# ScalarE issues half of the spreads of five norms' scales, and half of the first quarter's values in the first chunk

## The chip, the core and the metric

The kernel runs on one core of a Trainium2 chip. The metric is the device time of one execution in microseconds. The names of the engines in what follows are the profile's: PE (TensorE, matmuls) with PEld (its weight loads), DVE (VectorE), ACT (ScalarE), POOL (GpSimd), and SP (SyncE), which does no arithmetic here and issues the DMAs. "SPq" is SP's instruction queue: the time that its instructions take there.

## The reference

The input is x with 16 sequences of 512 tokens and 128 channels. A block with a recurrent attention (16 heads of 8 channels) and a feed-forward net is added to it, and then a small mixture of four experts:

```python
x = x + attn_block(_layernorm(x))
x = x + ffn_block(_layernorm(x))

# in attn_block
x = _ln(x, ln_pre_w, ln_pre_b)
xn = _ln(x, ln_attn_w, ln_attn_b)
r, k, v = xr @ W_r, xk @ W_k, xv @ W_v      # xr, xk, xv: xn mixed with its shift by one token
kk = kk / norm(kk)
def step(state, inp):                       # 512 steps, one after the other
    sa = einsum('bhij,bhj->bhi', state, a_t)
    state = state * d_t + sa * b_t + v_t * k_t
    return state, einsum('bhij,bhj->bhi', state, r_t)
x = x + (_gn_heads(o) + bonus) * g @ W_o
xf = _ln(x, ln_ffn_w, ln_ffn_b)
x = x + square(relu(kf @ W_ffn1)) @ W_ffn2

# in ffn_block: each token goes to the expert with the largest logit
y = _layer_norm(gelu(x @ W1[e] + b1[e]) @ Wo + bo + x)
```

## The kernel before

**Layout and chunks.** Channels lie on the 128 partitions. The 512 tokens are cut into 16 chunks of 32 steps. A chunk has 32 x 16 = 512 columns (step, sequence), and a step of the scan works on 8 x 16 = 128 columns.

**The order of the work.** Each engine's program is written out by hand. The tables `AT`, `AT_FIRST` (the first two chunks) and `AT_LAST` (the last two) give every piece of a chunk's work a place, counted in scan steps of that chunk: places below 0 lie in the iteration before, places from 32 on in those behind. In iteration i the engines scan chunk i, prepare chunk i+1 and finish chunks i-1 and i-2. At each step t an engine takes the scan's own instruction first and then, in `others()`, what the tables put there, the later chunk ahead of the earlier one. Every engine is strictly in order: an instruction that waits holds up all that stands behind it.

**A scan step.** DVE multiplies the state by `a_t` (`s_a`, L884), PE sums that over each head into `sa_ps` (L405), DVE multiplies the sums by `b_t` (`upd`, L894) and adds `plus_kv` (`state`, L898). POOL makes `plus_kv` (L1071) and multiplies the states by `r_t`. The products `kv` of keys and values are made by DVE (L871) eight steps ahead, one quarter of the chunk (8 steps) at a time, out of `val_rep0` and `val_rep1`, in which each value stands on all partitions of its head.

**PE's own filler.** Beside the needed matmuls PE runs the `keep` matmuls (L586), whose result nobody reads.

**The norms' scales.** A norm's variance is summed by PE in `sums` (L361) into a quarter of a bank, 32 partitions for each quarter of the columns. ACT makes the scale out of it with Ln and Exp on a tile of 128 x 128 (`rsqrt_row`, L618 and L620, the tile `row[name]`). Four DMAs, one for each quarter, then copy the 32 partitions to all 128 of `rs_p`, `rs_m` or `rs_f` (`over_channels`, L301). DVE multiplies by that. The norms are `rs0` and `rs1` (ahead of the attention, chunk i+1 in iteration i), `frs` (ahead of the feed-forward net, chunk i-1), `ers` (chunk i-1) and `lrs` (the experts' two, `lrs` of chunk i-2). `rk`, the scale of the keys, is spread in the same way (L298). The scale of the per-head norm of the scan's output is made by ACT in full width instead (`rs_m`, L609 and L611, the place `grs`) and needs no DMA.

**The values.** `replicate` (L314) issues eight DMAs for a quarter: each copies the 16 partitions of one value index of `val_c` to all 128.

**The queue of DMAs.** Every DMA is issued by SP, in order. In an iteration SP takes: the load of x, the values of quarters 1 and 2 of chunk i, the scales rs0 and rs1 (chunk i+1) and frs (chunk i-1), the values of quarter 3, rk, the values of quarter 0 of chunk i+1, the second load of x, lrs, ers and the store.

The lines that the prediction speaks of besides these: on ACT the decay's tanh (`dec_bt`, L679) and the tanh of `th_a` (`dx`, L683); the squares of the feed-forward net's hidden layer (`hid`, L757); the evacuations `val_c` (L696) and `val` (L701). On DVE the mix for the gate (`mix_g`, L926), which `th_a` waits for; the product with the per-head norm's scale (`y_m`, L962, the place `gxh`). On PE the first layer of the experts (`fin_a`, `fin_b`, L564) and the second layer of the feed-forward net (`mid_ps`, L515).

Of the kernel before, what the change touches and what calls it, by code (L numbers as in the profile page):

```python
# [13 lines left out]
H, N = 16, 8  # L14
# [4 lines left out]
QCOLS = QUARTER * B  # L19
# [93 lines left out]
class Chunk:  # L113


    def __init__(self, base, off):
        self.base, self.off = base, off
        self.slot = off % RING
        self.place = AT_FIRST if off < 2 else AT_LAST if off >= CHUNKS - 2 else AT

    def __add__(self, n):
        return Chunk(self.base, self.off + n)
# [18 lines left out]
def settled(eng, value):  # L141

    return value if isinstance(value, int) else eng.to_reg(value)


def build(nc, xT, mats, vecs, consts, b1_in, out):
    with ExitStack() as ctx:
        def sb(name, cols, dtype=F32, rows=128):
            return ctx.enter_context(nc.sbuf_tensor(name, [rows, cols], dtype))
# [4 lines left out]
        def single(name, cols):  # L154
            return [sb(name, cols)] * RING
# [4 lines left out]
        def sem(name):  # L160
            return ctx.enter_context(nc.semaphore(name))
# [31 lines left out]
        val_rep = [sb(f"val_rep{n}", N * QCOLS) for n in range(2)]  # L193
        val_scan = sb("val_scan", C)
        val_c = sb("val_c", COLS)
# [3 lines left out]
        sq_p, rs_p, xh_p = (sb(n, COLS) for n in ("sq_p", "rs_p", "xh_p"))  # L199
        row = {n: sb(f"row_{n}", QCOLS) for n in ("rs0", "rs1", "rk", "frs", "ers", "lrs")}  # L200
# [6 lines left out]
        rkb, kk, kki, inv_p, th_a = mix["k"], mix["v"], mix["g"], dec_bt, dx  # L207
# [7 lines left out]
        x2, sq_m, rs_m, y_m, z_m = (sb(n, COLS) for n in ("x2", "sq_m", "rs_m", "y_m", "z_m"))  # L215
# [3 lines left out]
        y1, y1b, y2, sq_f, rs_f = (sb(n, COLS) for n in ("y1", "y1b", "y2", "sq_f", "rs_f"))  # L219
        h = single("h", COLS)  # L220
# [25 lines left out]
        s = {n: sem("s_" + n) for n in names}  # L246
# [14 lines left out]
        def pipeline(eng, work, scan_step=None):  # L261

            def iteration(c):
                for t in range(STEPS):
                    def others():
                        for skew in range(-FIRST, CHUNKS - LAST - 2, -1):
                            if (c + skew).has():
                                work(c + skew, t - skew * STEPS)
                    if scan_step:
                        scan_step(c, t, others)  # L270
                    else:
                        others()

            for c in range(FIRST, LAST + 1):
                iteration(Chunk(0, c))


        @block.sync
        def _(sp):
            sp.dma_start(x_in[0][:], xT[:, 0:COLS]).then_inc(s["x_in"], 16)  # L280
            sp.dma_start(con[:], consts).then_inc(s["consts_in"], 16)
            sp.dma_start(vec[:], vecs).then_inc(s["consts_in"], 16)
            sp.dma_start(mat[:], mats).then_inc(s["w_in"], 16)
            sp.wait_ge(s["tiles"], 1)
            for n in range(3):
                sp.dma_start(b1_rows[32 * n:32 * n + E, :], b1_in).then_inc(s["b1_in"], 16)

            def over_channels(c, name, to, free=(), heads=None):

                waits = [(s[n], settled(sp, (c + back).count())) for n, back in free if c.has(-back)]  # L290
                now = settled(sp, c.count())
                for done, n in waits:
                    sp.wait_ge(done, n)
                sp.wait_ge(s["row_" + name], now)
                for g in range(4):
                    if heads:
                        rows = row[name][32 * g:32 * g + H, :].unsqueeze(1).broadcast_to([H, N, QCOLS])
                        sp.dma_start(to[:, g * QCOLS:(g + 1) * QCOLS], rows).then_inc(s[name], 16)  # L298
                    else:
                        rows = row[name][32 * g:32 * g + 32, :].unsqueeze(1).broadcast_to([32, 4, QCOLS])  # L300
                        sp.dma_start(to[:, g * QCOLS:(g + 1) * QCOLS], rows).then_inc(s[name], 16)  # L301

            def replicate(c, q):

                slot = q % 2
                free = c.count(2 * (q - 2) + 2, 2 * QUARTERS)
                free = free if isinstance(free, int) else settled(sp, free)
                now = settled(sp, c.count())
                if not isinstance(free, int) or free > 0:
                    sp.wait_ge(s["kv"], free)  # L310
                sp.wait_ge(s["val_c"], now)
                for i in range(N):
                    heads = val_c[i * H:(i + 1) * H, q * QCOLS:(q + 1) * QCOLS].unsqueeze(1).broadcast_to([H, N, QCOLS])
                    sp.dma_start(val_rep[slot][:, i * QCOLS:(i + 1) * QCOLS], heads).then_inc(s[f"val_rep{slot}"], 16)  # L314

            def work(c, at):
                for q in range(QUARTERS):
                    if at == c.place["rep"][q]:
                        replicate(c, q)
                if at == c.place["d_rs0"]:  # L320
                    over_channels(c, "rs0", rs_p, [("kk", -1)])
                if at == c.place["d_rs1"]:
                    over_channels(c, "rs1", rs_p, [("xh0", 0)])
                if at == c.place["d_rk"]:
                    over_channels(c, "rk", rs_p, [("xh1", 0)], heads=True)
                if at == c.place["d_frs"]:
                    over_channels(c, "frs", rs_m, [("gxh", 0)])
                if at == c.place["d_ers"]:
                    over_channels(c, "ers", rs_f, [("lxh", -1)])
                if at == c.place["d_lrs"]:  # L330
                    over_channels(c, "lrs", rs_f, [("h", 0)])
                if at == c.place["x_in"]:
                    if c.has(1):
                        sp.wait_ge(s["c0"], (c + -1).count())
                        sp.dma_start(x_in[c.slot][:], xT[:, c.cols(sp)]).then_inc(s["x_in"], 16)
                if at == c.place["x_res"]:
                    if c.has(1):
                        sp.wait_ge(s["x2x"], (c + -1).count())
                    sp.dma_start(x_res[c.slot][:], xT[:, c.cols(sp)]).then_inc(s["x_res"], 16)
                if at == c.place["store"]:  # L340
                    sp.wait_ge(s["res"], c.count())
                    sp.dma_start(out[:, c.cols(sp)], res[c.slot][:]).then_inc(s["stored"], 16)

            pipeline(nc.sync, work)
            sp.wait_ge(s["stored"], 16 * CHUNKS)
# [246 lines left out]
        def _(act):  # L592
# [20 lines left out]
            def rsqrt_row(c, var, eps, n_in, n_ln, name, scale=1.0):  # L613

                if c.has(1):
                    act.wait_ge(s[name], (c + -1).count(64, 64))
                act.wait_ge(s[n_in], c.count())
                f(row[name][:], var, ACT.Ln, bias=eps, scale=scale).then_inc(s[n_ln], 1)  # L618
                act.wait_ge(s[n_ln], c.count())
                f(row[name][:], row[name][:], ACT.Exp, scale=-0.5).then_inc(s["row_" + name], 1)  # L620

            def work(c, at):
                if at == c.place["sq0"]:
# [4 lines left out]
                if at == c.place["rs0"]:  # L628
                    tables(EXP)
                    rsqrt_row(c, pre_b[:, 0:QCOLS], eps_sq, "j0", "ln0", "rs0", scale=1.0 + 1e-5)  # L630
# [17 lines left out]
                if at == c.place["rs1"]:  # L648
                    tables(EXP)
                    rsqrt_row(c, pre_b[:, 0:QCOLS], eps_ln, "j1", "ln1", "rs1")  # L650
# [40 lines left out]
                if at == c.place["val_c"]:  # L691
                    act.wait_ge(s["v"], c.count())
                    if c.has(1):
                        act.wait_ge(s["val_rep0"], (c + -1).count(32 * N, 32 * N))
                        act.wait_ge(s["val_rep1"], (c + -1).count(32 * N, 32 * N))
                    f(val_c[:], pre_a[:], ACT.Identity).then_inc(s["val_c"], 1)  # L696
                if at == c.place["val_sb"]:
                    act.wait_ge(s["val_mm"], c.count())
                    if c.has(1):
                        act.wait_ge(s["bonus"], (c + -1).count())  # L700
                    f(val[:], pre_a[:], ACT.Identity).then_inc(s["val"], 1)  # L701
# [6 lines left out]
                if at == c.place["rk"]:  # L708
                    tables(EXP)
                    rsqrt_row(c, pre_b[:, 0:QCOLS], eps_kk, "kks", "lnk", "rk")  # L710
# [452 lines left out]
```

## Time and profile before

| | |
|---|---|
| median of 3 runs | 1193.74 us (1191.18 to 1196.12) |
| the profiled execution's own time | 1195.53 us |
| its span, first to last instruction | 1193.7 us |
| PE busy | 1054.8 us (88%) |
| DVE busy | 940.2 us (79%) |
| ACT busy | 605.3 us (51%) |
| POOL busy | 650.4 us (54%) |
| TensorE's mean granted clock | 0.968 of full speed |

An iteration in the middle takes 66.2 to 66.5 us. Busy times are those of arithmetic alone: SP's and ACT's time for issuing DMAs is not in them. In the rows of a timeline each row has the start, the time it took, engine, line, operation, what it writes and reads, its size, the count, and in brackets the idle time of the engine before it with what ended that. In the rows of the chain of work that ended last each piece has its start, its time, and what it was.

### The profile page before, as it was taken

The page shows a single profiled execution, that of the slowest core. Times are in us where ns is not written, and L with a number is a line of the kernel's source. Part 1 is how long each engine was busy: PE and PEld are TensorE (multiplying, and loading weights), DVE is VectorE, ACT ScalarE, POOL GpSimd, SP SyncE. Part 2 cuts the span into 40 slices and gives each one's busy share as a digit, 9 for nine tenths or more (in the row PEclk, how much of TensorE's full clock was granted, in tenths as well). Part 3 has the DMA queues.
Part 4 walks back from the last instruction along what each step waited for, and adds up shares of the span by engine and source line. Part 5 has one row for each costly group of instructions (what it writes and reads, how often), then busy time and mean ns, then how long its engine had stood idle before and what let it go on. Part 6 is the DMA issues. An engine that isn't in the chain of part 4 may idle for free.

```text
span 1193.7 us, 19599 instructions
## 1 busy us (share of the span) xinstructions
PE 1054.8 (88%) x6099; PEld 713.3 (60%) x6099; DVE 940.2 (79%) x2283; ACT 605.3 (51%) x965; POOL 650.4 (54%) x885
## 2 busy tenths in 40 slices
PE   4676689999998999999998989999999999988976
PEld 2243356666565757666665757566666656666755
DVE  4468778898989888898988888898889888876320
ACT  2424364736465574637464564647364654733341
POOL 0246665665656656566656666665556566555200
PEclk9769899999999999999999999999999999999989
DMA  3324123342424233432424232333425233221110
GB/s 126 67 40 75 33 45 71 63 89 42 100 47 86 56 61 69 78 72 52 94 42 96 56 74 56 67 71 62 90 41 102 45 84 57 52 58 36 37 27 18
DMA packets 136496, 75.58 MB, mean 63 GB/s; under 512 B 15292, under 2 KB 129980, under 8 KB 136264
## 3 DMA queue, kind: packets, MB, share of 16 engines
q1 hardware_dynamic: 136392, 74.33, 31.0%
q8 instruction: 49, 0.80, 0.3%
q14 instruction: 55, 0.45, 0.1%
HBM read 11.35 MB, written 4.19 MB: 13 GB/s over the span
## 4 chain that ended last, share of the span: by engine, by line
PE 36%; DVE 20%; SPq 19%; issue 10%; ACT 8%; DMA 6%; POOL 0%; DVEq 0%; ACTq 0%; POOLq 0%
SPq L314 10%; SPq L301 6%; PE fin_b L564 6%; PE fin_a L564 5%; DMA val_rep<-val_c 5%; PE sa_ps L405 5%; DVE state L898 4%; PE mid_ps L356 4%; PE pre_a L356 3%; DVE upd L894 3%; PE var_ps L586 3%; ACT L600 3%; SPq L298 3%; DVE kv L871 2%; DVE s_a L884 1%
## 5 line engine op out<-in xcount | busy, mean ns | idle before, releaser
L1071 POOL TENSOR_TENSOR plus_kv<-state,kv 128x128 f32<-128x128 f32 x512 | 283.3, 553 | 406.1 <-DVE state L898 383.1
L405 PE MATMUL sa_ps<-s_a,con 128*128 128x128 f32 x1024 | 226.0, 303 | 55.8 <-DVE s_a L884 53.2
L405 PEld LDWEIGHTS sa_ps<-s_a,con 128*128 128x128 f32 x1024 | 172.3, 193 | 168.7 <-DVE s_a L884 137.7
L1063 POOL TENSOR_TENSOR s_r<-state,r_t 128x256 f32<-128x256 f32 x256 | 244.7, 956 | 3.3 <-DVE state L898 3.3
L894 DVE TENSOR_TENSOR upd<-sa_ps,b_t 128x128 f32<-128x128 f32 x512 | 146.2, 286 | 84.6 <-PE sa_ps L405 80.7
L898 DVE TENSOR_TENSOR state<-upd,plus_kv 128x128 f32<-128x128 f32 x512 | 191.8, 375 | 17.6
L884 DVE TENSOR_TENSOR s_a<-state,a_t 128x128 f32<-128x128 f32 x512 | 149.4, 292 | 18.5
L564 PE MATMUL fin_b<-h_e,mat 128*128 128x256 f32 x512 | 136.9, 394 | 4.0 <-ACT pick L770 4.0
L871 DVE TENSOR_TENSOR kv<-val_rep,k_t 128x512 f32<-128x512 f32 x128 | 117.8, 921 | 23.9 <-DMA val_rep<-val_c 23.3
L600 ACT ACT_TABLE_LOAD x101 | 129.6, 1283 | 1.8
L564 PE MATMUL fin_a<-h_e,mat 128*128 128x256 f32 x512 | 127.9, 379 | 0.0
L586 PE MATMUL var_ps<-con 128*128 128x256 f32 x416 | 120.7, 400 | 0.0
L564 PEld LDWEIGHTS fin_b<-h_e,mat 128*128 128x128 f32 x512 | 91.6, 192 | 35.9 <-issue 23.9
L564 PEld LDWEIGHTS fin_a<-h_e,mat 128*128 128x128 f32 x512 | 93.1, 190 | 22.8 <-issue 13.4
L586 PEld LDWEIGHTS var_ps<-con 128*128 128x128 f32 x416 | 75.4, 200 | 30.3 <-issue 26.3
L770 ACT ACTIVATE pick<-fin_b 68x512 bf16<-68x512 bf16 x16 | 9.5, 592 | 142.5 <-PE fin_b L548 142.5
L574 PE MATMUL fin_b<-act,mat 128*128 128x256 f32 x256 | 71.4, 385 | 0.0
L515 PE MATMUL mid_ps<-hid,mat 128*128 128x256 f32 x256 | 64.6, 385 | 0.0
L574 PEld LDWEIGHTS fin_b<-act,mat 128*128 128x128 f32 x256 | 47.4, 190 | 17.4 <-ACT act L777 10.1
L515 PEld LDWEIGHTS mid_ps<-hid,mat 128*128 128x128 f32 x256 | 46.3, 190 | 14.9 <-ACT hid L757 9.9
L762 ACT ACTIVATE sq_f<-fin_a 128x512 f32<-128x512 f32 x16 | 9.6, 597 | 81.2 <-PE fin_a L356 81.2
L398 PE MATMUL o_ps<-s_r,con 128*32 128x128 f32 x1024 | 41.7, 281 | 0.3 <-POOL s_r L1063 0.3
(198 smaller groups left out, 1725.9 us busy)
## 6 DMA issues: line engine op xcount, KB each, us to landing
val_rep<-val_c SPq DMA_DIRECT2D x512, 64.0 KB, 2.4
rs_p<-row_rs SPq DMA_DIRECT2D x128, 64.0 KB, 2.1
x_in<-xT SPq DMA_DIRECT2D x16, 256.0 KB, 3.0
rs_p<-row_rk SPq DMA_DIRECT2D x64, 64.0 KB, 2.4
x_res<-xT SPq DMA_DIRECT2D x16, 256.0 KB, 3.0
rs_m<-row_frs SPq DMA_DIRECT2D x64, 64.0 KB, 2.1
rs_f<-row_ers SPq DMA_DIRECT2D x64, 64.0 KB, 2.1
rs_f<-row_lrs SPq DMA_DIRECT2D x64, 64.0 KB, 2.1
```

What stands on the lines that cost most here:

```text
L314: sp.dma_start(val_rep[slot][:, i * QCOLS:(i + 1) * QCOLS], heads).then_inc(s[f"val_rep{slot}"], 16)
L405: mm(sa_ps[:, 0:STATE], k("sum8"), s_a[:], start=True, stop=True).then_inc(s["sa"], 1)
L564: mm(to[:, half(part)], mat[:, M["W1"] + e * I + j * C:M["W1"] + e * I + (j + 1) * C], h_e[e][:, half(part)], start=(e == 0 and part == 0) ...
L574: last = mm(fin_b[:, half(part)], w("Wo", j), act_j[j][:, half(part)], start=(j == 0 and part == 0), stop=(j == J - 1), skip_group_check=True)
L586: mm(var_ps[:, 2 * C:4 * C], k("sum8"), con[:, 0:2 * C], start=True, stop=True, skip_group_check=True)
L600: nc.scalar.preload_act_table_set(name)
L871: tt(part, values.rearrange("p (i t b) -> p i t b", i=N // 2, t=QUARTER), keys.unsqueeze(1).broadcast_to([128, N // 2, QUARTER, B]), ALU.m ...
L884: tt(ib(s_a[:]), ib(st(t)), over_i(a_t[c.slot][:, t * B:(t + 1) * B]), ALU.mult).then_inc(s["s_a"], 1)
L894: tt(ib(upd[:]), ib(sa_ps[:, 0:STATE]), over_i(b_t[c.slot][:, t * B:(t + 1) * B]), ALU.mult).then_inc(s["upd"], 1)
L898: tt(st(t + 1), upd[:], plus_kv[:, (t % 2) * STATE:(t % 2 + 1) * STATE], ALU.add).then_inc(s["state"], 1)
L1063: tt(part, states, r.unsqueeze(2).broadcast_to([128, 2, N, B]), ALU.mult).then_inc(s["s_r"], 1)
L1071: tt(plus_kv[:, (t % 2) * STATE:(t % 2 + 1) * STATE], st(t), kv[:, at:at + STATE], ALU.add).then_inc(s["plus_kv"], 1)
```

## The change

In five norms ScalarE issues the DMAs of the last two quarters itself, right behind the Exp that makes the scale, and SP issues the first two. ScalarE has to wait for its own Exp before it issues, and for the last reader of the tile that it writes into. In the first chunk ScalarE also issues the last four of the eight DMAs of the values' first quarter, right behind `val_c`. SP keeps all four DMAs of rk and all eight of every other quarter.

```diff
@@ class Chunk
+        self.by_act = {"rs0", "rs1", "frs", "ers", "lrs"} | ({"rep"} if off == 0 else set())
@@ over_channels (SP)
-                for g in range(4):
+                for g in range(2 if name in c.by_act else 4):
@@ replicate (SP)
-                for i in range(N):
+                for i in range(N // 2 if q == 0 and "rep" in c.by_act else N):
@@ rsqrt_row (ScalarE), behind its Exp
+                if name in c.by_act:
+                    to, read, back = {"rs0": (rs_p, "kk", 1), "rs1": (rs_p, "xh0", 0),
+                                      "frs": (rs_m, "gxh", 0), "ers": (rs_f, "lxh", 1), "lrs": (rs_f, "h", 0)}[name]
+                    if c.has(back):
+                        act.wait_ge(s[read], (c + -back).count())
+                    act.wait_ge(s["row_" + name], c.count())
+                    for g in (2, 3):
+                        rows = row[name][32 * g:32 * g + 32, :].unsqueeze(1).broadcast_to([32, 4, QCOLS])
+                        nc.scalar.dma_start(to[:, g * QCOLS:(g + 1) * QCOLS], rows).then_inc(s[name], 16)
@@ work (ScalarE), behind val_c
+                    if "rep" in c.by_act:
+                        act.wait_ge(s["val_c"], c.count())
+                        for i in range(N // 2, N):
+                            heads = val_c[i * H:(i + 1) * H, 0:QCOLS].unsqueeze(1).broadcast_to([H, N, QCOLS])
+                            nc.scalar.dma_start(val_rep[0][:, i * QCOLS:(i + 1) * QCOLS], heads).then_inc(s["val_rep0"], 16)
```

The first place is on ScalarE, at steps 3 to 5 of an iteration in the middle: the scale rs0 of chunk i+1 and the full-width scale `rs_m` of chunk i-1 (names in brackets are the semaphores waited for; line numbers of the changed kernel are 2 to 16 higher). Before:

```order
L730 ACTIVATE sq_m<-o_ps 128x512 [waits s_fj,s_o]
L600 ACT_TABLE_LOAD
L618 ACTIVATE row_rs<-pre_b,eps_sq 128x128 [waits s_j0,s_rs0]
L620 ACTIVATE row_rs<-row_rs 128x128 [waits s_ln0]
L609 ACTIVATE rs_m<-mid_ps,eps_gn 128x512 [waits s_gj]
L611 ACTIVATE rs_m<-rs_m 128x512 [waits s_gln]
```

and after:

```order
L746 ACTIVATE sq_m<-o_ps 128x512 [waits s_fj,s_o]
L602 ACT_TABLE_LOAD
L620 ACTIVATE row_rs<-pre_b,eps_sq 128x128 [waits s_j0,s_rs0]
L622 ACTIVATE row_rs<-row_rs 128x128 [waits s_ln0]
L631 DMA rs_p<-row_rs 128x1x128 [waits s_row_rs0,s_kk]
L631 DMA rs_p<-row_rs 128x1x128
L611 ACTIVATE rs_m<-mid_ps,eps_gn 128x512 [waits s_gj]
L613 ACTIVATE rs_m<-rs_m 128x512 [waits s_gln]
```

Two issues of DMAs now stand between the scale rs0 and the two instructions that make `rs_m`.

The second place is on ScalarE too, at steps 9 and 10: the scales frs of chunk i-1 and rs1 of chunk i+1. Before:

```order
L600 ACT_TABLE_LOAD
L618 ACTIVATE row_frs<-var_ps,eps_ln 128x128 [waits s_fj,s_frs]
L620 ACTIVATE row_frs<-row_frs 128x128 [waits s_fln]
L618 ACTIVATE row_rs<-pre_b,eps_ln 128x128 [waits s_j1,s_rs1]
L620 ACTIVATE row_rs<-row_rs 128x128 [waits s_ln1]
```

and after:

```order
L620 ACTIVATE row_frs<-var_ps,eps_ln 128x128 [waits s_fj,s_frs]
L622 ACTIVATE row_frs<-row_frs 128x128 [waits s_fln]
L631 DMA rs_m<-row_frs 128x1x128 [waits s_row_frs,s_gxh]
L631 DMA rs_m<-row_frs 128x1x128
L620 ACTIVATE row_rs<-pre_b,eps_ln 128x128 [waits s_j1,s_rs1]
L622 ACTIVATE row_rs<-row_rs 128x128 [waits s_ln1]
L631 DMA rs_p<-row_rs 128x1x128 [waits s_row_rs1,s_xh0]
```

The issues of frs stand ahead of the Ln and Exp of rs1, so that rs1 is made later.

The third place is SP's queue at steps 9 to 11: rs1, frs and the values of quarter 3. Before:

```order
L301 DMA rs_p<-row_rs 128x1x128 [waits s_row_rs1,s_xh0]
L301 DMA rs_p<-row_rs 128x1x128 x3
L301 DMA rs_m<-row_frs 128x1x128 [waits s_row_frs,s_gxh]
L301 DMA rs_m<-row_frs 128x1x128 x3
L314 DMA val_rep<-val_c 128x1x128 [waits s_val_c,s_kv]
L314 DMA val_rep<-val_c 128x1x128 x7
```

and after:

```order
L303 DMA rs_p<-row_rs 128x1x128 [waits s_row_rs1,s_xh0]
L303 DMA rs_p<-row_rs 128x1x128
L303 DMA rs_m<-row_frs 128x1x128 [waits s_row_frs,s_gxh]
L303 DMA rs_m<-row_frs 128x1x128
L316 DMA val_rep<-val_c 128x1x128 [waits s_val_c,s_kv]
L316 DMA val_rep<-val_c 128x1x128 x7
```

Four issues fewer stand ahead of the values of quarter 3.

## Rows read from the trace of the kernel before

**Rows 1.** The page: busy time, and the chain that ended last by engine.

```profile
PE 1054.8 (88%) x6099; PEld 713.3 (60%) x6099; DVE 940.2 (79%) x2283; ACT 605.3 (51%) x965; POOL 650.4 (54%) x885
...
PE 36%; DVE 20%; SPq 19%; issue 10%; ACT 8%; DMA 6%; POOL 0%; DVEq 0%; ACTq 0%; POOLq 0%
```

**Rows 2.** The chain that ended last, one iteration, rs1 to the values' landing.

```profile
608.10 0.54 SPq L301
...
613.53 0.57 SPq L314
...
618.04 2.38 DMA val_rep<-val_c
```

**Rows 3.** The waits, whole trace: in total, times, longest.

```profile
DVE kv L871 <- DMA val_rep<-val_c: 23.3, 28, 3.2
...
DVE y_m L962 <- ACT rs_m L611: 4.4, 13, 2.1
```

**Rows 4.** ScalarE's timeline, the same iteration, steps 9 to 19.

```profile
607.12 0.31 ACT L620 ACTIVATE row_frs<-row_frs 128x128 f32<-128x128 f32 x1
607.34 0.35 ACT L618 ACTIVATE row_rs<-pre_b,eps_ln 128x128 f32<-128x128 f32 x1
...
621.62 1.15 ACT L679 ACTIVATE dec_bt<-pre_a,half_w 128x512 f32<-128x512 f32 x1 [0.56 <-PE pre_a L356]
623.03 0.69 ACT L683 ACTIVATE dx<-pre_b,half_a 128x512 f32<-128x512 f32 x1 [0.26 <-DVE mix_g L926]
```

**Rows 5.** VectorE's timeline at the first product with quarter 3's values.

```profile
620.51 0.69 DVE L871 TENSOR_TENSOR kv<-val_rep,k_t 128x512 f32<-128x512 f32 x1 [0.98 <-DMA val_rep<-val_c]
```

**Rows 6.** ScalarE's timeline in the next iteration, from rs0 to `rs_m`.

```profile
660.89 0.31 ACT L620 ACTIVATE row_rs<-row_rs 128x128 f32<-128x128 f32 x1
661.11 0.67 ACT L609 ACTIVATE rs_m<-mid_ps,eps_gn 128x512 f32<-128x512 f32 x1
```

**Rows 7.** VectorE's timeline behind it.

```profile
662.47 0.69 DVE L962 TENSOR_TENSOR y_m<-o_ps,rs_m 128x512 f32<-128x512 f32 x1 [0.19 <-ACT rs_m L611]
...
663.72 0.29 DVE L884 TENSOR_TENSOR s_a<-state,a_t 128x128 f32<-128x128 f32 x1
```

**Rows 8.** TensorE's timeline behind that.

```profile
662.68 1.89 PE L564 MATMUL fin_a<-h_e,mat 128*128 128x256 f32 x8
664.41 0.38 PE L405 MATMUL sa_ps<-s_a,con 128*128 128x128 f32 x2
```

**Rows 9.** ScalarE's timeline, the last hidden square behind lrs (step 28).

```profile
635.87 0.63 ACT L757 ACTIVATE hid<-hid 128x512 f32<-128x512 f32 x1
```

**Rows 10.** TensorE's timeline, the matmuls that read the hidden layer's last two parts.

```profile
637.09 1.89 PE L515 MATMUL mid_ps<-hid,mat 128*128 128x256 f32 x8
```

**Rows 11.** The chain that ended last, start of the program.

```profile
13.45 2.13 DMA rs_p<-row_rs
...
53.50 3.11 DMA x_in<-xT
```

**Rows 12.** ScalarE's timeline, start of the program, around `val_c`.

```profile
40.26 0.58 ACT L696 ACTIVATE val_c<-pre_a 128x512 f32<-128x512 f32 x1
43.01 0.60 ACT L701 ACTIVATE val<-pre_a 128x512 f32<-128x512 f32 x1 [2.17 <-PE pre_a L356]
```

**Rows 13.** TensorE's timeline, start of the program.

```profile
17.27 2.07 PE L356 MATMUL pre_a<-x,con 128*128 128x512 f32 x2 [0.83 <-ACT x L635]
...
53.73 0.49 PE L405 MATMUL sa_ps<-s_a,con 128*128 128x128 f32 x2 [1.53 <-DVE s_a L884]
...
56.66 2.08 PE L356 MATMUL pre_a<-x_in,con 128*128 128x512 f32 x2 [0.84 <-DMA x_in<-xT]
```

**Rows 14.** The last hidden square of the last chunk on ScalarE's timeline.

```profile
1144.27 0.63 ACT L757 ACTIVATE hid<-hid 128x512 f32<-128x512 f32 x1
```

**Rows 15.** TensorE's matmuls that read it, last chunk.

```profile
1144.05 2.03 PE L515 MATMUL mid_ps<-hid,mat 128*128 128x256 f32 x8
```

**Rows 16.** The chain that ended last, end of the program.

```profile
1187.65 2.13 DMA rs_f<-row_lrs
```

## The prediction, made before the changed kernel ran

> **What bounds the kernel now.** I read the page first. PE is busy 88% of the span, and the chain that ended last spends 36% on PE, 20% on DVE and 19% in SP's queue [rows 1]. So two things must be seen beside each other: PE, which has little room left, and SP's issuing of DMAs. The chain of one iteration shows SP's part: rs1's first issue starts at 608.10, the values of quarter 3 start at 613.53, their eighth issue at 618.04, and they land 2.38 us later [rows 2]. One issue therefore costs SP (618.04 - 613.53) / 7 = 0.64 us, and the eight issues of rs1 and frs take 613.53 - 608.10 = 5.4 us. The list of waits then tells how much of that reaches anybody: DVE waited for values 28 times, 23.3 us in all, the longest 3.2 us [rows 3]. The timelines of ScalarE, VectorE and TensorE tell who passes a delay on.
>
> The change removes about 2.6 us of SP's queue ahead of quarter 3, and gives ScalarE ten issues per iteration. ScalarE is busy 51% [rows 1], but what counts is what stands behind each pair of issues.
>
> **Price of an issue on ScalarE.** No row shows one. The nearest row is SP's, of the same shape: 0.54 to 0.57 us for the first of a group and 0.64 in steady sequence [rows 2]. I take 1.25 us for a pair with the wait ahead of it. The bounds are nothing (ScalarE hands the work over) and 2.6 us (the two queues take turns, so that a pair lasts as long as SP's four do now).
>
> **Quarter 3 (gain).** Before, the Exp of frs starts at 607.12 and the Ln of rs1 at 607.34, overlapped [rows 4]. After, the Ln waits until the Exp is through (607.43) and the pair is issued: 608.7, 1.35 us later, and so is rs1's row. SP saves 4 x 0.64 = 2.6 us behind that, so quarter 3 starts and lands 1.2 us earlier. The product `kv` waited 0.98 us for it [rows 5], so DVE gains that 0.98. What is late next: the gate's mix comes 0.98 earlier, but `th_a` (L683) waited only 0.26 us for it and stands on ScalarE behind the decay's tanh, 621.62 + 1.15 = 622.77, which waited for PE [rows 4]. **0.3 us per iteration is left.** The spread of rs1 itself lands when it did: 1.35 later, two issues earlier.
>
> **The per-head norm (loss).** Behind rs0's Exp (660.89 + 0.31 = 661.20) stands the Ln that makes `rs_m`. It started at 661.11, and after the change at 661.20 + 1.25 = 662.45, which is 1.34 us later [rows 6]. DVE's product `y_m` waited for `rs_m` (0.19 us) before [rows 7], as in 13 iterations [rows 3], so the 1.34 us pass to DVE whole. Queued behind it on DVE are `upd`, `state` and the next `s_a` at 663.72, ready at 664.01. It becomes ready at 665.35. PE wants it at 664.41, between two runs of eight experts' matmuls [rows 8]: the cover is 0.4 us, and PE then stands for 665.4 - 664.41 = 1.0 us with its filler and the experts' matmuls queued behind. PE runs without a gap before and after, so **1.0 us is lost per iteration.** rs0's own spread lands 1.3 us earlier, for nobody: its reader has its place four steps later.
>
> **lrs and ers.** The pair of lrs moves the last hidden square from 635.87 to about 637.2, ready at 637.9 [rows 9]. PE reads it in the second half of the run that starts at 637.09, at 637.09 + 1.89 / 2 = 638.0 [rows 10]. Cost: nothing, with 0.1 us of cover; each 0.1 us by which a pair costs more than 1.25 us is lost in full. ers: the pair moves the gate's tanh, which has a similar margin; nothing.
>
> **Iterations.** rs0 meets `rs_m` in iterations 1 to 14. In iteration 1 the order of rs1 and frs on ScalarE is the other way round (chunk 0's table), and rs1's spread is waited for there: two issues less bring about 1.3 us, which I set against that iteration's 1.3. The other 13 give 13 x (1.0 - 0.3) = **+9.1 us.**
>
> **The start.** An isolated spread ends with its fourth issue at 13.45 and 2.13 us of landing [rows 11]; with two issues each it ends 1.3 us earlier. For rs0, PE's next matmul waited 0.83 us [rows 13], so 0.8 is gained (filler stands before it); for rs1 the full 1.3. For quarter 0's values SP issues four fewer, but ScalarE issues four behind `val_c` (40.26 + 0.58 = 40.84, plus 2.55 = 43.4), so `val` at 43.01 comes 0.4 late [rows 12]. PE's first scan matmul waited 1.53 us for DVE, which waited for these values [rows 13]; of that 1.53 - 0.4 = 1.1 is gained. The second chunk's x was issued at 53.50 behind SP's sixteen value DMAs, landing 3.11 later [rows 11]; four fewer take away the 0.84 us that PE waited [rows 13]. Sum: 0.8 + 1.3 + 1.1 + 0.84 = **-4.1 us.**
>
> **The end.** In the last chunk the spreads of ers and lrs stand alone in the chain (lrs: fourth issue at 1187.65, 2.13 to land [rows 16]): -2 x 1.3. Against it, the last hidden square ends at 1144.27 + 0.63 = 1144.90 [rows 14], becomes ready at 1146.15, and PE wants it at 1144.05 + 2.03 / 2 = 1145.07 [rows 15]: +1.0, and about as much in the same place of the chunk before. **-0.6 us.**
>
> **Sum.** +9.1 - 4.1 - 0.6 = +4.4 us. The profiled execution took 1195.53 us, so it would take 1199.9; the median of the runs is 1193.74, and I predict **1198 us.** A measurement of this kernel can tell about 0.5%, or 6 us, from no change.
>
> **A rule weighed.** The rows show 0.64 us of queue per DMA against 2.13 to 2.38 us to land [rows 2, 11], so four issues are worth more than a landing, and saving issue time is worth something. The Trainium skill speaks against the change here (DMA: Bandwidth & Descriptors, section Issuing engines are not separate DMA queues): issuing from several engines saves only the sequencer's time, "which is usually small relative to the DMA itself". By that rule the gains would be near 0 and the losses of 15 x 1.0 us would stand alone; the trace disagrees on "small". The Trainium skill also has the opposite advice (Perfetto Trace Analysis, section DMA Optimizations): where descriptor generation is the bottleneck, balancing DMAs over engines may help. That is the side of the first rival.
>
> **Rivals.**
> - *ScalarE issues almost for nothing, or PE absorbs the stall.* For it: no row shows an issue on ScalarE. Against it: ScalarE must wait for its Exp to end and then issue in order, and the same shape costs SP 0.64 [rows 2]. Then +13 goes away: 14 x 0.3 gained, -4.1 and -2.6: 1183 us, faster. It decides at a pair of about 0.95 us: there the loss is 15 x 0.7 (13 iterations and the two at the end), as large as the gains of 10.6.
> - *The two queues take turns on something they share.* For it: nothing shown, but SP's issues come at an even 0.64 however short the queue. Then a pair beside SP's pair takes 2.6 us: the stall at `rs_m` is 2.3 us, and lrs loses 1.3 more: 13 x (1.3 + 1.3) = +34, with the ends about +38 over the forecast: 1236 us.
> - *Small margins fail.* A pair costs 1.5 to 1.6 us, so that rs_m, lrs and the gate's tanh each lose 0.3: 13 x 0.7 = +9: 1207 us.
>
> **Chances.** Forecast 0.52, of which its own spread of 0.35 us per iteration (plus or minus 5 us) leaves some beyond +6; small margins fail 0.22; cheap or absorbed 0.18; taking turns 0.08. Faster by over 0.5%: the cheap case, 0.18. Slower by over 0.5%: the last two and a part of the forecast's own, 0.38. Within: 0.44. The range leaves out the shared queue's case and the far half of the cheap one: 1184 to 1211 us.
>
> **What the changed profile would show.** ScalarE's pair at about 1.2 us behind each Exp; `y_m` waiting some 1.5 us for `rs_m` in 13 iterations, and PE waiting 1.0 us for `s_a` right behind; `kv` of quarter 3 no longer waiting; an iteration of 66.9 to 67.1 us instead of 66.4; the scan's first matmul on PE at about 50.5 instead of 53.73; the last lrs spread 1.3 us shorter. The prediction is wrong if the pair costs much less or more than 1.25 us, or if PE doesn't stall behind `y_m`.

## The result, and the profile after

The changed kernel takes 1218.15 us (median of 4 runs, 1217.28 to 1221.4), the kernel before 1193.72 us in the runs beside it: a ratio of 1.0187, 95% interval 1.0166 to 1.0208. It is slower by 1.9%, some 24 us. The forecast was 1198 us with a range of 1184 to 1211: the direction came out, the size did not, and the time lies outside the range. The profiled execution has a span of 1215.7 us against 1193.7.

The page of the changed kernel, busy time and the chain that ended last by engine, answers to [rows 1]:

```profile
PE 1062.6 (87%) x6099; PEld 713.6 (59%) x6099; DVE 948.1 (78%) x2283; ACT 606.2 (50%) x965; POOL 659.2 (54%) x885
...
PE 42%; DVE 22%; ACT 12%; issue 10%; SPq 5%; ACTq 3%; DMA 3%; POOL 0%; DVEq 0%; POOLq 0%
```

SP's queue fell from 19% of the chain to 5%. In its place stand ScalarE (8% to 12%), ScalarE's own issuing (0% to 3%) and more of PE and DVE. The instructions are as many as before (6099 on PE, 2283 on DVE) and their busy time grew by under 1%; the chain moved. The list of waits of the changed kernel (in total, times, longest) says where, and answers to [rows 3]:

```profile
PE sa_ps L407 <- DVE s_a L900: 70.8, 115, 2.7
...
ACT L602 <- issue: 45.4, 29, 1.6
...
DVE y_m L978 <- ACT rs_m L613: 27.9, 15, 2.1
...
ACT rs_m L611 <- issue: 22.5, 14, 1.6
ACT hid L771 <- issue: 21.5, 15, 1.6
...
DVE kv L887 <- DMA val_rep<-val_c: 8.3, 10, 2.0
```

Two groups of [rows 3] changed sides: the products with the values now wait 8.3 us in all, not 23.3, and `y_m` waits 27.9 us, not 4.4. The rows that end in "issue" are ScalarE standing still for the pairs it issues: 1.6 us at the longest, where 1.25 was forecast.

**The norm per head, iteration 9.** ScalarE's timeline, from rs0's Exp to `rs_m`, answers to [rows 6]:

```profile
670.72 0.31 ACT L622 ACTIVATE row_rs<-row_rs 128x128 f32<-128x128 f32 x1
671.12 1.47 ACTq L631 DMA_DIRECT2D rs_p<-row_rs  x2
672.64 0.69 ACT L611 ACTIVATE rs_m<-mid_ps,eps_gn 128x512 f32<-128x512 f32 x1 [1.61 <-issue]
```

The pair takes 1.47 us, and it begins 0.09 us after the Exp has ended. Before, the Ln started 0.22 us behind the start of the Exp [rows 6]; now 1.92 behind it. So `rs_m` is 1.70 us late, not 1.34. VectorE's timeline behind it, which answers to [rows 7]:

```profile
674.02 0.69 DVE L978 TENSOR_TENSOR y_m<-o_ps,rs_m 128x512 f32<-128x512 f32 x1 [1.90 <-ACT rs_m L613]
...
675.27 0.29 DVE L900 TENSOR_TENSOR s_a<-state,a_t 128x128 f32<-128x128 f32 x1
675.48 0.94 DVE L984 SCALAR_TENSOR_TENSOR z_m<-y_m,vec,bonus 128x512 f32<-128x512 f32 x1
...
676.66 1.26 DVE L914 TENSOR_TENSOR state<-upd,plus_kv 128x128 f32<-128x128 f32 x1
677.95 0.29 DVE L900 TENSOR_TENSOR s_a<-state,a_t 128x128 f32<-128x128 f32 x1
```

and TensorE's, which answers to [rows 8]:

```profile
672.52 1.89 PE L566 MATMUL fin_a<-h_e,mat 128*128 128x256 f32 x8
675.62 0.49 PE L407 MATMUL sa_ps<-s_a,con 128*128 128x128 f32 x2 [1.21 <-DVE s_a L900]
...
677.67 0.38 PE L569 MATMUL fin_a<-pick,b_all 68*128 68x512 bf16 x1
678.29 0.49 PE L407 MATMUL sa_ps<-s_a,con 128*128 128x128 f32 x2 [0.24 <-DVE s_a L900]
```

PE waits at the place that was forecast, and then again one step later, which was not. From the first run of eight to the first `sa_ps` it takes 675.62 - 672.52 = 3.10 us, where it took 664.41 - 662.68 = 1.73 before [rows 8]: 1.37 lost. The next step shows the rest. VectorE's and TensorE's timelines of the kernel before, one step after [rows 7, 8]:

```profile
665.16 1.21 DVE L898 TENSOR_TENSOR state<-upd,plus_kv 128x128 f32<-128x128 f32 x1
666.40 0.29 DVE L884 TENSOR_TENSOR s_a<-state,a_t 128x128 f32<-128x128 f32 x1
```

```profile
666.75 0.49 PE L405 MATMUL sa_ps<-s_a,con 128*128 128x128 f32 x2
```

There `s_a` ended at 666.69 and PE took it at 666.75: no slack at all. From one `sa_ps` to the next it took PE 666.75 - 664.41 = 2.34 us, after the change 678.29 - 675.62 = 2.67: another 0.33. Together 1.70 us, exactly what `rs_m` is late. The 0.4 us of cover at the first `sa_ps` was real, but only lent: DVE runs without a gap from `y_m` through two steps (`z_m` behind the first `s_a`, and in the second step a `state` of 1.2 us), and PE meets it again, with nothing to spare, at the end of them.

**Quarter 3, iteration 8** (ScalarE's pair for frs, the product with quarter 3's values on VectorE, the gate's tanh on ScalarE), which answers to [rows 4, 5]:

```profile
617.74 1.21 ACTq L631 DMA_DIRECT2D rs_m<-row_frs  x2
```

```profile
629.76 0.94 DVE L887 TENSOR_TENSOR kv<-val_rep,k_t 128x512 f32<-128x512 f32 x1
```

```profile
632.92 0.65 ACT L694 ACTIVATE dx<-pre_b,half_a 128x512 f32<-128x512 f32 x1
```

The product no longer waits (0.98 before [rows 5]) and neither does `th_a` (0.26 before [rows 4]). This pair took 1.21 us, and SP issued nothing beside it: its next issue starts at 619.83.

**By step, whole trace.** The scan's step is a clock for the whole program: each step's `s_a` on VectorE is found in both timelines. The table is worked out from them: how much later (+) each iteration starts in the changed kernel, and how much it loses (+) or gains (-) in its parts. Seven iterations are left out; the sums have all sixteen.

```
iteration    starts  steps   step    steps   steps   steps   steps    step
             later   0-6     6-7     7-15    15-17   17-26   26-30    30-next
 0           -2.28   -1.45    0.00   -0.55   -0.32    0.12   -0.05    0.01
 1           -4.52    0.06    1.31    0.90   -0.57   -0.51   -0.01    0.02
 2           -3.32   -0.01    1.49   -0.35    0.94   -0.25    0.00    0.01
 3           -1.49    0.00    1.73   -0.01    0.65    0.00    0.00    0.01
 8            8.51    0.00    1.71    0.00    0.08   -0.47    0.00    0.01
12           13.60   -0.49    1.71    0.00    0.06   -0.40   -0.46    0.13
13           14.15   -0.01    1.72    0.00    0.04   -0.35    0.01    1.52
14           17.08    0.00    1.72   -0.01    0.02   -0.07    0.25    1.42
15           20.41    0.00    0.01    0.00    0.01   -0.01    2.99   -0.01
all 16               -1.87   23.38   -0.05    1.53   -4.61    3.26    4.04
```

Step 6 to 7, where `y_m` stands, loses 23.38 us, more than the 22.0 by which the span grew; all else nearly cancels.

Three pieces of such a table come and go from one kernel's execution to the next, touched by the change or not, and the long ones have the lower mean granted clock. Steps 0 to 6 of iteration 0 took 12.5 to 12.7 us at a clock of 0.60 (the kernel before, experiments 4 and 9) and 10.1 to 11.6 at 0.79 to 1.00 (all others). Steps 0 to 6 of iteration 2 took 12.1 at 1.00 and 13.7 at 0.88 (experiments 3, 4 and 6). Steps 7 to 15 of iteration 15 took 18.5 at 1.00 (before, changed, experiments 1, 4 and 5) and 19.7 at 0.91 (the other seven). Differences of 1 to 2 us at these places say nothing of the change. Step 6 to 7 is not one of them.

### The profile page after: what moved, and what is told of

It is laid out like the page before. It is cut to its first block, busy times and chain, and to the rows that moved or that the text cites. A ratio compares the mean times of both kernels' runs of the same rounds, so it can differ in the third digit from the quotient of the medians.

```text
span 1215.7 us, 19677 instructions
## 1 busy us (share of the span) xinstructions
PE 1062.6 (87%) x6099; PEld 713.6 (59%) x6099; DVE 948.1 (78%) x2283; ACT 606.2 (50%) x965; POOL 659.2 (54%) x885
## 4 chain that ended last, share of the span: by engine, by line
PE 42%; DVE 22%; ACT 12%; issue 10%; SPq 5%; ACTq 3%; DMA 3%; POOL 0%; DVEq 0%; POOLq 0%
PE sa_ps L407 6%; PE fin_b L566 6%; DVE state L914 6%; PE fin_a L566 5%; DVE upd L910 4%; PE pre_a L358 4%; PE var_ps L588 4%; SPq L316 4%; ACT L602 3%; ACTq L631 3%; PE fin_b L576 3%; PE mid_ps L358 3%; DVE s_a L900 2%; PE pre_b L358 2%; DMA val_rep<-val_c 2%
## 5 line engine op out<-in xcount | busy, mean ns | idle before, releaser
L1079 POOL TENSOR_TENSOR s_r<-state,r_t 128x256 f32<-128x256 f32 x256 | 253.6, 990 | 3.3 <-DVE state L914 3.3
L914 DVE TENSOR_TENSOR state<-upd,plus_kv 128x128 f32<-128x128 f32 x512 | 194.8, 381 | 17.6
L900 DVE TENSOR_TENSOR s_a<-state,a_t 128x128 f32<-128x128 f32 x512 | 150.3, 294 | 18.5
L887 DVE TENSOR_TENSOR kv<-val_rep,k_t 128x512 f32<-128x512 f32 x128 | 120.7, 943 | 8.3 <-DMA val_rep<-val_c 8.3
L773 ACT ACTIVATE hid<-hid 128x512 f32<-128x512 f32 x64 | 40.3, 630 | 2.0
```

The source lines that it names most:

```text
L887: tt(part, values.rearrange("p (i t b) -> p i t b", i=N // 2, t=QUARTER), keys.unsqueeze(1).broadcast_to([128, N // 2, QUARTER, B]), ALU.m ...
L900: tt(ib(s_a[:]), ib(st(t)), over_i(a_t[c.slot][:, t * B:(t + 1) * B]), ALU.mult).then_inc(s["s_a"], 1)
L914: tt(st(t + 1), upd[:], plus_kv[:, (t % 2) * STATE:(t % 2 + 1) * STATE], ALU.add).then_inc(s["state"], 1)
L1079: tt(part, states, r.unsqueeze(2).broadcast_to([128, 2, N, B]), ALU.mult).then_inc(s["s_r"], 1)
```

## The experiments

Each is an edit of `by_act`, the set of spreads that ScalarE shares, if nothing else is said. "Alone" means the kernel before with this part of the change.

**1. All but rs0.**

```diff
-        self.by_act = {"rs0", "rs1", "frs", "ers", "lrs"} | ({"rep"} if off == 0 else set())
+        self.by_act = {"rs1", "frs", "ers", "lrs"} | ({"rep", "rs0"} if off == 0 else set())
```

> The changed kernel, but SP alone issues rs0's spread in all chunks except the first. Theory (the loss is rs0's pair standing ahead of rs_m on ScalarE): the 1.7 us that step 6 to 7 gained in each of 14 iterations goes away, so 1218 - 14 x 1.7 = 1194 us, y_m waits for rs_m 0.2 to 0.4 us again, and an iteration takes 66.3 us. Rival (the issues of ScalarE's queue slow everything by contention, wherever they stand, or the pairs of rs1, frs, ers and lrs cost as much): less than half of it comes back, 1206 us or more.

Measured: 1198.59 us, ratio 1.0041 (1.0022 to 1.0061). In the profiled execution `y_m` waited 4.4 us in all, as before, and step 6 to 7 was the same to 0.01 us. The theory has the place right; the time is 4.6 us above it. Experiments 8 and 9 suggest why: the pairs of ers and lrs cost more than the changed kernel's table let one see. The profiled execution is the fastest of six (1193.38 to 1201.76).

**2. rs0 alone.**

```diff
+        self.by_act = {"rs0"} if off > 0 else set()
```

> The kernel before, and of the change rs0's pair alone, in chunks 1 and later (nothing in the first). Theory: ScalarE's pair takes 1.45 us beside SP's, rs_m is 1.7 us late, PE waits for s_a, 14 iterations x 1.7 = +24: 1217 us. Rival (the loss is shared between the pairs, and SP's two issues less give some of it back): 1205 us or less.

Measured: 1220.33 us, ratio 1.0219 (1.0198 to 1.024), 24.9 us above the kernel before. Step 6 to 7 lost 23.47 us over the trace, 1.70 to 1.72 in each of iterations 3 to 14, and the rest of the trace nearly cancels (the scan ends 24.75 us later). One pair per iteration is the whole slowdown.

**3. The same, behind `rs_m`.** ScalarE issues rs0's pair after the Ln and the Exp of `rs_m`, in iterations 1 to 14. (Shown is the call; `pair` is the code of the pair, taken out of `rsqrt_row`.)

```diff
                 if at == c.place["grs"]:
                     tables(EXP)
                     rsqrt(c, mid_ps[:], eps_gn, rs_m[:], rs_m[:], "gj", "gln", "grs")
+                    if (c + 2).has(0):
+                        pair(c + 2, "rs0")
```

> As the run with rs0's pair alone, but ScalarE issues the pair behind the two activations that make rs_m instead of ahead of them (in iterations 1 to 14). As many issues by as many engines, about 1.3 us later. Theory (order: rs_m stands behind the pair on an engine that works in order): y_m waits 0.2 to 0.4 us again, PE doesn't stall for s_a, and the time is that of the kernel before, 1194 to 1197 us. Rival (the issues cost by contention or by a queue shared with SP, wherever they stand): 1210 us or more.

Measured: 1195.53 us, ratio 0.9991 (0.9977 to 1.0006). ScalarE's timeline of this kernel:

```profile
593.99 0.31 ACT L622 ACTIVATE row_rs<-row_rs 128x128 f32<-128x128 f32 x1
594.20 0.67 ACT L611 ACTIVATE rs_m<-mid_ps,eps_gn 128x512 f32<-128x512 f32 x1
594.90 0.63 ACT L613 ACTIVATE rs_m<-rs_m 128x512 f32<-128x512 f32 x1
594.97 1.24 ACTq L636 DMA_DIRECT2D rs_p<-row_rs  x2
596.23 1.28 ACT L602 ACT_TABLE_LOAD   x1 [0.70 <-issue]
```

The same two issues, and the 24.9 us are gone. It is the order on ScalarE that costs, not the issues. The pair starts here while the Exp ahead of it still runs (594.97 against 595.53), because it waits for rs0's row, which is long done, and not for that Exp; ScalarE stands still for 0.70 us, not 1.6, in front of a table load that nobody waits for.

**4. SP's pair later.** As experiment 2, but SP issues its own two only when ScalarE has gone on to `rs_m`.

```diff
                 sp.wait_ge(s["row_" + name], now)
+                if name == "rs0" and c.has(2):
+                    sp.wait_ge(s["gln"], settled(sp, (c + -2).count()))
```

> As the run with rs0's pair alone, but SP issues its own pair only when ScalarE has gone on to rs_m, so that the two pairs don't overlap. Theory (the second issue of ScalarE's pair takes 0.85 instead of 0.6 us because SP issues at the same time): the pair takes 1.21 us, rs_m is 0.26 us earlier, 14 x 0.26 = 3.6 us less than 1220: 1216 to 1217 us. Rival (0.85 us is the price of a second issue right behind a first on ScalarE): the pair stays at 1.46 us and the time at 1220 us.

Measured: 1213.73 us (1210.64 to 1216.05), ratio 1.0136 (1.0109 to 1.0162). ScalarE's and SP's timelines:

```profile
604.89 1.21 ACTq L633 DMA_DIRECT2D rs_p<-row_rs  x2
606.15 0.69 ACT L613 ACTIVATE rs_m<-mid_ps,eps_gn 128x512 f32<-128x512 f32 x1 [1.34 <-issue]
```

```profile
606.92 1.21 SPq L305 DMA_DIRECT2D rs_p<-row_rs  x2
```

ScalarE's pair takes 1.21 us in 13 of 15 chunks, where experiment 2 had 1.47 in 13, and step 6 to 7 loses 1.45 us, where it lost 1.71. The two engines' issuing does disturb each other, by 0.26 us for two against two: far from taking turns (2.6 us), not nothing. The spans of the two profiled executions (1218.1 and 1214.2 us) are 3.9 us apart, as the theory has it. The medians, each against the kernel before beside it, are 7.4 apart (24.9 and 17.5 above it), and where the other 3.5 us went is open.

**5. One issue, not two.** As experiment 2, with one issue by ScalarE and three by SP.

```diff
-                for g in range(2 if name in c.by_act else 4):
+                for g in range(3 if name in c.by_act else 4):
...
-                    for g in (2, 3):
+                    for g in (3,):
```

> As the run with rs0's pair alone, but ScalarE issues one of rs0's four and SP three. It tells what PE's cover at step 6 to 7 is worth. One issue takes 0.6 us with 0.15 to go on, so rs_m is 0.85 us late. Theory (no cover: the step's path lies on DVE and GpSimd, so that all of it is lost, as with the pair, where 1.70 late gave 1.71): 14 x 0.85 = +12: 1207 us. Rival (PE has 0.4 us of cover, as predicted): 14 x 0.45 = +6: 1201 us.

Measured: 1205.06 us, ratio 1.0077 (1.0053 to 1.0102). VectorE's and TensorE's timelines:

```profile
666.95 0.69 DVE L978 TENSOR_TENSOR y_m<-o_ps,rs_m 128x512 f32<-128x512 f32 x1 [1.02 <-ACT rs_m L613]
```

```profile
668.55 0.49 PE L407 MATMUL sa_ps<-s_a,con 128*128 128x128 f32 x2 [0.32 <-DVE s_a L900]
...
671.23 0.49 PE L407 MATMUL sa_ps<-s_a,con 128*128 128x128 f32 x2 [0.24 <-DVE s_a L900]
```

`y_m` is 1.02 - 0.19 = 0.83 us later than in [rows 7], and step 6 to 7 lost 0.81 to 0.84 us in each of iterations 3 to 14. With 0.4 us of cover it would have lost 0.4. The median (8.8 us above the kernel before) lies between the two forecasts, the steps are plain: **late by 0.83, 1.45 and 1.70 us gave a loss of 0.83, 1.45 and 1.71.** The 0.24 us at the second `sa_ps` is the same in this kernel and in the changed one: what is lost there is the cover of the first, however late `rs_m` is.

**6. frs and rs1 alone.**

```diff
+        self.by_act = {"rs1", "frs"}
```

> The kernel before, and of the change the pairs of frs and rs1 alone, in every chunk. Theory: quarter 3's values come 1.2 us earlier, th_a 0.3 us earlier, which is 0.2 to 0.3 us per iteration, and 1.3 at the start: 14 x 0.25 + 1.3 = 5 us less, 1189 us. Rival (the gain is eaten by rs1's and frs's place on ScalarE): 1192 to 1196 us.

Measured: 1191.69 us, ratio 0.9971 (0.9956 to 0.9985): 3.7 us less. Steps 17 to 26 gain 3.3 us over the trace, 0.35 per iteration, but iterations 2 and 3 lose 1.3 and 0.8 us at steps 15 to 17. ScalarE's and TensorE's timelines in iteration 2:

```profile
209.93 1.46 ACTq L631 DMA_DIRECT2D rs_m<-row_frs  x2
211.41 1.28 ACT L602 ACT_TABLE_LOAD   x1 [1.57 <-issue]
212.71 0.60 ACT L793 ACTIVATE act<-fin_b 128x512 f32<-128x512 f32 x1
```

```profile
213.36 0.70 PE L576 MATMUL fin_b<-act,mat 128*128 128x256 f32 x2 [1.57 <-ACT act L793]
```

The first chunks have another table of places, and there frs's pair stands ahead of an expert's activation that PE wants at once. It is the mistake of rs0 again, in two iterations.

**7. The two ends.**

```diff
+        self.by_act = {"rs0", "rs1", "frs", "rep"} if off == 0 else {"ers", "lrs"} if off == CHUNKS - 1 else set()
```

> ScalarE issues halves in the first chunk (rs0, rs1, frs and quarter 0's values) and in the last (ers, lrs), and in no other. Theory: the start gives 4.5 us as in the changed kernel, the end 1.4 us (the last hidden square may give 1 back), and nothing between changes: 1188 us. Rival (what the start gains is lost again by the next iterations, since the scan's steady state catches up with a wait that the start had hidden): 1191 to 1194 us.

Measured: 1188.89 us, ratio 0.9953 (0.9936 to 0.997). In the profiled execution iteration 1 starts 6.2 us earlier and that stays to the end of the scan (6.1), and 2.1 us come at the tail: the span is 1185.5. What the start gains is not lost again. A part of the 6.2 is the slow start of the kernel before in its profiled execution (see the start, below). The medians give 6.5 us for both ends (interval 3.6 to 7.7); the forecast's terms for them come to 4.1 + 2.6 - 1.0 = 5.7.

**8. ers and lrs alone, in every chunk.**

```diff
+        self.by_act = {"ers", "lrs"}
```

> The kernel before, and of the change the pairs of ers and lrs alone, in every chunk. Theory (the two have small margins that fail in some iterations: the gate's tanh behind ers in iterations 13 and 14, the last hidden square behind lrs in 14 and 15): +1.5 x 2 +3, and 2 x 1.4 back at the end, 1197 to 1200 us. Rival (their pairs cost nothing, as predicted, and the end gains): 1193 us or less.

**9. lrs alone, in every chunk.**

```diff
+        self.by_act = {"lrs"}
```

> The same with lrs's pair alone, in every chunk. Theory: the last hidden square loses about 2.6 us in iteration 15 and something in a few others, 1.3 us come back at the end: 1195 to 1197 us, so ers costs the rest of the run with both. Rival (lrs carries the loss): within 1 us of the run with both.

Measured: 1204.01 us, ratio 1.0076 (1.0053 to 1.0099), and 1201.81 us, ratio 1.0052 (1.0036 to 1.0068). Both are above what was expected: 9 and 7 us above the kernel before, where 3 to 6 and 1 to 3 were. The rival of the last run is nearer: lrs carries most. Its scan ends 6.35 us later in the profiled execution. 3.0 of that is the hidden square in iteration 15, as below. Another 1.2 is at steps 7 to 15 of iteration 15, where kernels without this pair lose it too. The tail adds 1.5, though lrs's last spread is shorter there; in the kernels that leave the last chunk as it was it adds between -0.4 and +1.1. Another 2.6 come in small pieces at steps 26 to 28 of iterations 4 to 14, from +1.0 to -0.5; experiments 2, 3, 5, 6 and 7, which leave lrs there to SP, have -1.0 to +1.3 in the same place. In iteration 8 it is this, SP's queue and VectorE of the run with lrs alone:

```profile
630.70 6.11 SPq L316 DMA_DIRECT2D val_rep<-val_c  x8
```

```profile
639.24 0.69 DVE L887 TENSOR_TENSOR kv<-val_rep,k_t 128x512 f32<-128x512 f32 x1 [1.89 <-DMA val_rep<-val_c]
```

Quarter 0's values land later than before, so that `kv` waits 1.89 us where it waited 0.81. ScalarE issued its pair at 636.08, inside the last of SP's value issues; before, SP itself issued lrs behind them. That the pair's transfers get between the values' is my reading of these rows. It was not tried by itself, and the scatter in the kernel before (quarter 0's eight issues took 5.78 and 5.95 us in two iterations, other quarters' 5.1) makes a part of it chance. So the medians show that lrs's pair costs some 7 us (interval 4 to 8), and the rows account for the hidden square alone; the rest is open.

**10. What the others point to.** The two ends, frs from chunk 3 and rs1 from chunk 5 on.

```diff
+        self.by_act = {"rs0", "rs1", "frs", "rep"} if off == 0 else set()
+        if off >= 3:
+            self.by_act = self.by_act | {"frs"}
+        if off >= 5:
+            self.by_act = self.by_act | {"rs1"}
+        if off == CHUNKS - 1:
+            self.by_act = self.by_act | {"ers", "lrs"}
```

> The first chunk's pairs and the last chunk's (the run of both ends), and besides frs's pair from chunk 3 and rs1's from chunk 5 on, which spares the iterations 2 and 3 that lost in the run of frs and rs1. Theory: the gains add up, 1189 minus 10 x 0.35 = 1185.5 us. Rival (PE takes the 0.35 us back elsewhere once the start is earlier): 1188 to 1189 us.

Measured: 1183.77 us, ratio 0.9897 (0.9875 to 0.9918): faster than the kernel before by 1.0%, and by 34 us than the changed one. Steps 17 to 26 gain 3.6 us, iterations 2 and 3 lose nothing, and an iteration takes 65.88 us (66.33 before, 67.90 in the changed kernel). It is the same change with the harmful places left out.

## Why the prediction was wrong

**What failed: "the cover is 0.4 us ... 1.0 us is lost per iteration".** The forecast followed the delay from `rs_m` over `y_m` to the first `sa_ps`, found 0.4 us of slack there, and stopped. DVE had no gap up to the next `s_a`, and PE no slack at it (0.06 us), so the slack was given back one step later. Experiments 4 and 5 show it: whatever `rs_m` is late is lost whole. The forecast took 1.34 - 1.0 = 0.34 us off in each iteration: 14 x 0.34 = 4.8 us of the miss.

**Mis-sized: the price of the pair.** 1.25 us was forecast, 1.47 measured, and 1.61 from the Exp's end until ScalarE goes on. Alone it would be 1.21 (experiment 4), so the price taken from SP's rows was right for an engine that issues by itself; SP's own pair of the same spread beside it adds 0.26 us. The lateness is 1.70, not 1.34: 14 x 0.36 = 5.0 us. With both, the step lost 23.4 us where the forecast had 13 x 1.0. (The fourteenth, iteration 1, was set against a gain of 1.3 from rs1's earlier spread. It did not come: iteration 1 loses 1.2 us in all, and without rs0's pair, in experiment 1, it gains nothing.) **This term is 10 us of the 17.6 by which the growth of the span missed the forecast** (22.0 against 4.4), and experiment 2 shows that it alone makes a slowdown as large as the whole. The gate's tanh, frs's pair and the end, below, make up most of the rest.

**Right: quarter 3 gains 0.3 us per iteration.** Measured 0.35 to 0.47 at steps 17 to 26, 4.6 us over the trace against 13 x 0.3 = 3.9, for the reason given: `kv` stops waiting and `th_a` loses its small wait.

**The start: 4.1 us forecast, 4.5 measured, in part by luck.** The row foretold was not there: the first `sa_ps` comes at 52.49, not at 50.5. VectorE's first `s_a` starts 2.28 us earlier than before (51.11 against 53.39), but PE comes to it 1.1 us after its end. The granted clock was 0.72 from 50 to 53 us, where the kernel before had 1.00. So 1.2 us of the gain are there at that `sa_ps`, and the other 3.3 come in the steps behind it, where the kernel before had the lower clock: its steps 0 to 6 are one of the three pieces that come and go. Seven kernels leave the first chunk as it was, the one before and experiments 2 to 5, 8 and 9. Against the kernel before, their iteration 1 starts between 0.4 us later and 2.9 earlier, on average 1.4 earlier. In the four that share all its issues (the changed kernel, experiments 1, 7 and 10) it starts 4.5 to 6.3 earlier, on average 5.3. These averages are 3.9 us apart, so the size of the sum holds; its four terms were not tried one by one. TensorE's timeline:

```profile
52.49 0.38 PE L407 MATMUL sa_ps<-s_a,con 128*128 128x128 f32 x2
```

**Wrong: "lrs and ers: nothing".** The gate's tanh had no margin in iterations 13 and 14. ScalarE's and TensorE's timelines of the changed kernel:

```profile
991.50 1.45 ACTq L631 DMA_DIRECT2D rs_f<-row_ers  x2
992.98 1.28 ACT L602 ACT_TABLE_LOAD   x1 [1.57 <-issue]
994.28 0.60 ACT L732 ACTIVATE th_g<-pre_b 128x512 f32<-128x512 f32 x1
```

```profile
994.93 1.12 PE L358 MATMUL pre_b<-th_g,mat 128*128 128x512 f32 x2 [1.83 <-ACT th_g L732]
```

That is 1.5 + 1.4 = 2.9 us, and eight iterations in the middle lose 0.13 more at the same place: 4.0 in all. frs's pair cost 1.6 us in iterations 2 and 3, in front of an expert's activation (experiment 6), which the forecast did not name. These are iterations in which chunks with another table of places take part than in the one that the forecast was worked out on.

**The end, in part.** The last lrs spread, in the chain of the changed kernel, answers to [rows 16]:

```profile
1208.75 0.58 ACTq L631
...
1209.36 2.38 DMA rs_f<-row_lrs
```

From the Exp's end to the landing it takes 1211.74 - 1208.68 = 3.06 us instead of 4.40: 1.3 less, as forecast. (ers: 3.20 instead of 4.10.) Against it the last hidden square was forecast to cost 1.0 in each of the last two chunks. In the last, PE waited 1.58 us for it; in the one before it cost 3.0. TensorE's timeline in both, the row of the kernel before that answers to the second, and a window of the changed kernel (its length, then busy time and count of PE, PEld, DVE, ACT and POOL, granted clock, DMA share, GB/s):

```profile
1121.64 1.13 PE L517 MATMUL mid_ps<-hid,mat 128*128 128x256 f32 x4 [1.14 <-ACT hid L773]
1123.56 2.08 PE L358 MATMUL fin_a<-y,con 128*128 128x512 f32 x2 [0.79 <-DVE y L1007]
...
1170.10 1.13 PE L517 MATMUL mid_ps<-hid,mat 128*128 128x256 f32 x4 [1.58 <-ACT hid L773]
```

```profile
1101.72 1.12 PE L356 MATMUL fin_a<-y,con 128*128 128x512 f32 x2 [0.78 <-DVE y L991]
```

```profile
1123.60:1126.60 3.00, 3.00 (x16) 1.71 (x20) 0.97 (x3) 0.60 (x1) 0.00 (x0) 0.50 0.00 0
```

The wait of 1.14 us is the forecast. Then `fin_a` takes 2.08 us where it took 1.12, since TensorE's granted clock stood at 0.50 (1.2 of 2.4 GHz) for 3 us right after the two waits, and the matmuls behind it are slower too. The clock's part is not in every execution: in experiments 1 and 8, with the same pair at the same place, steps 26 to 30 of iteration 15 took 11.15 us at a clock of 1.00, in the changed kernel and experiment 9 12.73 at 0.87, before 9.75. So the wait costs 1.4 and the clock 1.6. From the scan's end to the program's the kernel gains 1.4, so the end is +3.0 - 1.4 = +1.6 us, not -0.6.

**The rivals.** "Small margins fail" was nearest: it had the pair near 1.5 us, and `rs_m`, the gate's tanh and the hidden square lose, as it said. But it priced `rs_m` on the same cover of 0.4 us, so it stopped at 1207. "The queues take turns" was wrong in size, 0.26 and not 1.3 us. "Absorbed" was wrong: nothing was.

**The rule that was weighed.** By the Trainium skill (DMA: Bandwidth & Descriptors, section Issuing engines are not separate DMA queues), issuing from several engines saves only the sequencer's time, which is "usually small relative to the DMA itself". The runs show that time to be 0.6 us an issue beside 2.1 to 2.4 us from an issue's start to its landing, and sharing the issues where ScalarE has room for them to be worth 1.0% (experiment 10). What decided this case is another thing: the second engine pays for the issues with its own order of work.

## What to carry to other kernels

A DMA issue handed to a compute engine is an instruction in that engine's order (0.6 us for one here, 1.2 to 1.5 for two), so ask at every place, in the first and last iterations too, what stands behind it, and put it behind what others wait for: that alone was worth 25 us. Slack found at the first reader of a late tile need not be cover; follow the delayed engine until it has idle time of its own, and take the smallest slack up to there. An edit with many places is judged by place: one pair lost 25 us, two gained 4, two lost 9, the ends gained 7, and the good ones together are 1.0% faster than before.

## What the runs showed of the hardware that I had not expected

- Two issues on ScalarE take 1.21 us alone (experiment 4) and 1.47 beside a pair of SP's that starts at the same time (671.10 and 671.12). Where SP's pair starts 0.60 us ahead (experiment 3) they take 1.24. SP's pair takes 1.21 each time.
- An issue on ScalarE starts while an activation ahead of it still runs, if it doesn't wait for that one: 594.97 against an end at 595.53 (experiment 3). ScalarE then stands still for 0.70 us, not 1.6.
- ScalarE's DMAs land later when SP issues beside them, SP's own do not. From issue to landing the median is 2.39 us for ScalarE's DMAs of rs0 and rs1 in the changed kernel, and 2.13 for its DMAs of rs0 in experiment 4. SP's take 2.12 to 2.13 in both. At the end of the program that is 2.38 instead of 2.13 for lrs and 2.52 instead of 2.16 for ers.
- The granted clock differs between executions of the same instructions. Experiments 2 and 4 are alike up to the first scan step; from 20 to 40 us it was 1.00 in the one and 0.66 to 0.82 in the other, and the first `s_a` starts at 53.99 and at 50.94.
